# Three PSUM banks in turn for keys, values and expert products, and a new order for VectorE's side work

## What is computed

```
x = x + tanh(g_xattn[0]) * xattn0(ctx, layernorm(x), mask)      # 8 heads of 64
x = x + tanh(g_ffn[0])   * moe(layernorm(x))                    # 8 experts, 2 for each token
x = x + tanh(g_xattn[1]) * xattn1(ctx, layernorm(x), mask)      # 16 heads of 64
x = x + tanh(g_ffn[1])   * ffn1(layernorm(x))                   # 8-bit rows, ternary weights,
                                                                # depthwise convolution over 3 tokens, silu
```

## Time and profile before

| | |
|---|---|
| median of three runs | 1717.39 us |
| profiled execution: its own time | 1729.88 us |
| its span, first to last instruction | 1728.0 us |
| mean granted TensorE clock | 0.919 of full speed |
| TensorE busy | 1329.0 us, 77% |
| VectorE busy | 1171.2 us, 68% |
| ScalarE busy | 978.1 us, 57% |
| GpSimd busy | 867.0 us, 50% |

### The profile page before, as it was taken

One profiled execution on the slowest core, in us unless ns is written; L12 is line 12 of the kernel. 1 busy time (PEld: TensorE's weight loads), 2 busy tenths in 40 slices (PEclk: granted clock), 3 DMA queues, 4 the chain that ended last, 5 costly groups with the idle time before them and its releaser, 6 DMA issues.

```text
span 1728.0 us, 45307 instructions
## 1 busy us (share of the span) xinstructions
PE 1329.0 (77%) x16918; PEld 1016.7 (59%) x16918; DVE 1171.2 (68%) x3155; ACT 978.1 (57%) x2319; POOL 867.0 (50%) x1157
## 2 busy tenths in 40 slices
PE   2477777769888888788999888778777877877764
PEld 1355555547766766567877766555555655655553
DVE  4376768776655666656676667777777777767766
ACT  3466667446645666455545456556556655655651
POOL 4477667677755754555454443434333333433320
PEclk9798889889998999899999999999989999989985
DMA  4979978278999854479999963334234334423330
GB/s 130 255 187 187 222 166 201 64 194 202 242 203 234 198 82 91 108 188 210 236 235 241 227 150 64 72 80 85 61 76 88 67 69 80 80 66 72 72 61 9
DMA packets 443131, 239.97 MB, mean 139 GB/s; under 512 B 388784, under 2 KB 425760, under 8 KB 434336
## 3 DMA queue, kind: packets, MB, share of 16 engines
q1 hardware_dynamic: 407100, 172.49, 49.4%
q10 hardware_dynamic: 32740, 57.24, 11.0%
q0 software_dynamic: 3072, 7.34, 1.6%
HBM read 107.78 MB, written 35.50 MB: 83 GB/s over the span
## 4 chain that ended last, share of the span: by engine, by line
PE 28%; DVE 23%; ACT 14%; issue 10%; DMA 8%; POOL 8%; DVEq 5%; SPq 3%; ACTq 2%; another core or an unknown queue 0%; POOLq 0%
PE bank_keys L945 6%; PE bank_values L958 5%; ACT scores L740 4%; PE bank_hidden L995 4%; PE bank_x L1056 4%; POOL probs L580 3%; ACT probs L747 3%; DMA expert_up<-experts_up 3%; DMA probs_turned<-probs 3%; DVE scores L1205 3%; PE bank_out L977 2%; PE bank_scores L920 2%; DVE keys L1217 2%; ACT keys L760 2%; DVE values L1222 2%
## 5 line engine op out<-in xcount | busy, mean ns | idle before, releaser
L580 POOL TENSOR_TENSOR probs<-scores,probs 112x487 f16<-112x487 f32 x384 | 434.3, 1147 | 492.5 <-ACT probs L747 489.4
L740 ACT ACTIVATE scores<-scores,score_min 112x487 f32<-112x487 f32 x384 | 265.8, 694 | 182.1 <-DVE score_min L1205 181.0
L945 PE MATMUL bank_keys<-kv_B,weights 128*128 128x488 f16 x768 | 199.6, 401 | 102.6 <-DVE keys L1217 102.5
L1205 DVE CUSTOM_DVE_ANT_0 scores<-bank_scores,mask 112x487 f32<-112x487 f32 x384 | 238.7, 659 | 15.6 <-PE bank_scores L920 13.2
L958 PE MATMUL bank_values<-weights,kv_B 128*128 128x128 f16 x3072 | 199.2, 223 | 53.2 <-DVE values L1222 52.3
L747 ACT ACTIVATE probs<-scores 112x487 f16<-112x487 f32 x384 | 214.0, 605 | 24.1 <-DMA probs_turned<-probs 6.9
L958 PEld LDWEIGHTS bank_values<-weights,kv_B 128*128 128x128 f16 x3072 | 181.3, 100 | 73.5 <-DVE values L1222 72.9
L977 PE MATMUL bank_out<-values,probs_turned 128*128 128x64 f16 x4608 | 172.2, 195 | 8.7 <-DMA probs_turned<-probs 5.0
L1222 DVE SCALAR_TENSOR_TENSOR values<-bank_values,values 128x512 f16<-128x512 f32 x192 | 132.0, 687 | 62.7 <-ACT values L766 62.1
L945 PEld LDWEIGHTS bank_keys<-kv_B,weights 128*128 128x128 f16 x768 | 71.2, 103 | 174.7 <-DVE keys L1217 110.0
L977 PEld LDWEIGHTS bank_out<-values,probs_turned 128*128 128x128 f16 x4608 | 160.6, 100 | 10.6 <-issue 7.3
(11 more groups left out here) (225 smaller groups left out, 2382.8 us busy)
## 6 DMA issues: line engine op xcount, KB each, us to landing
expert_up<-experts_up SPq DMA_DIRECT2D x43, 1024.0 KB, 5.4
expert_down<-experts_down SPq DMA_DIRECT2D x43, 512.0 KB, 6.7
raw_weights<-in_weights ACTq DMA_DIRECT2D x8, 1536.0 KB, 10.6
experts_up<-expert_up ACTq DMA_DIRECT2D x8, 1024.0 KB, 5.5
raw_weights<-in_weights ACTq DMA_DIRECT2D x6, 1024.0 KB, 8.2
probs_turned<-probs SPq DMA_TRANSPOSE x384
context_turned_B<-kv_B ACTq DMA_DIRECT2D x16, 375.0 KB, 7.3
kv_B<-context_turned_B ACTq DMA_DIRECT2D x16, 375.0 KB, 3.8
```

The lines of the kernel that those rows point to most:

```text
L580: pool.tensor_tensor(PR[:, u % 4, 1, 0:KEYS], S[:, u % 4, 0:KEYS], PR[:, u % 4, 0, 0:KEYS], ALU.subtract).then_inc(probs_split, 1)
L740: act_e.activation(S[:, u % 4, 0:KEYS], S[:, u % 4, 0:KEYS], ACT.Exp, bias=rmin[:, u % 4:u % 4 + 1], scale=-1.0, accum_out=rsum[:, g % 2, ...
L945: last = pe.matmul(bK[:, 0:KW], w(wk + kb * step, a, 128 * (j % 4), 128), kv[layer][:, n % 2, kb, b, 0:KW], start=i == 0, stop=i == 5)
L1205: dve.tensor_tensor_reduce(out=S[:, u % 4, 0:KEYS], in0=bS[u % 2][0:TOK, 0:KEYS], in1=mask[:, m, 0:KEYS], scale=1.0, scalar=3.0e38, op0=AL ...
```

## The change

It has three parts.

1. **A ring of three banks.** Keys, values and the two expert halves take `bank_ring_0`, `_1`, `_2` in the order in which TensorE writes them (`ring_uses`). A use waits until the one three places before it has been read. Without experts this means that keys j+2 wait for the split of values j-2, and values j for the split of keys j+1. Three banks replace three, none is added.
2. **Evictions lag a place.** VectorE and ScalarE handle the `late` tasks of step j-1 in step j, not those of step j at its end. `split_k(j + 1)` comes right after the masks of step j, before it was `split_k(j + 2)` near the end of step j. `split_v(j - 1)` follows later; beside experts (`with_experts`) the values are split in their own step. VectorE does the `early` tasks behind its side work, ScalarE does them ahead of `round_probs`. The heads' and router's tasks come a step later where `slack` is 1 (all groups but two).
3. **The side work is dealt anew.** The tasks of the norms, the quantising and the convolution move to other steps, all still on VectorE. The eight taps of the convolution now stand in steps 18 and 19 of a sequence, before four in each of steps 16 to 19. The spill of a context to DRAM is issued a step later, the store of an expert tile a step earlier but behind the transposes.

```diff
+RING = 3
+def ring_uses():
+    uses = []
+    for j in range(FIRST_STEP, LAST_STEP + 1):
+        m = micro(j)
+        if is_pair(j + 2):
+            uses.append(("k", j + 2))
+        if m[0]:
+            uses.append(m[0])
+        if is_pair(j):
+            uses.append(("v", j))
+        if m[2]:
+            uses.append(m[2])
+    return uses
...
+            def ring_free(*use):
+                i = RING_AT[use] - RING
+                if i < 0:
+                    return
+                last = RING_USES[i]
+                if last[0] == "k":
+                    pe.wait_ge(k_split, last[1] + 1)
+                elif last[0] == "v":
+                    pe.wait_ge(v_split, last[1] + 1)
+                else:
+                    pe.wait_ge(gated, 2 * tile(last[1], last[2]) + last[3] + 1)
...
-                pe.wait_ge(k_split, j)
+                ring_free("k", j)
...
-                pe.wait_ge(v_split, j)
+                ring_free("v", j)
...
@@ early(j)
+    for n in range(NSEQ):
+        if j == start_b(n) + 26:
+            tasks.append(("f_down", n))
...
@@ late(j), where at = j - start_b(n)
-        if at == 14:
+        if at == 16:
             tasks.append(("f_turn", n))
-        if at == 15:
-            tasks.append(("f_up", n, 0))
-        if at == 24:
-            tasks.append(("f_max", n, 1))
-        if at == 27:
-            tasks.append(("f_down", n))
+        if at in (17, 18):
+            tasks.append(("f_up", n, at - 17))
+        if at in (20, 21):
+            tasks.append(("f_max", n, at - 20))
+        if at == 22:
+            tasks.append(("f_rate", n))
...
@@ ScalarE
-                if (j + 3) % 4 == 0 and 0 <= (j + 3) // 4 < NSEQ:
-                    spill_context((j + 3) // 4)
+                if (j + 2) % 4 == 0 and 0 <= (j + 2) // 4 < NSEQ:
+                    spill_context((j + 2) // 4)
...
+                for t in early(j):
+                    part(t)
                 if is_pair(j):
                     act_e.drain()
                     round_probs(2 * j)
                     round_probs(2 * j + 1)
                 load_weights(j)
-                for t in early(j):
+                for t in late(j - 1):
                     part(t)
...
@@ VectorE
-                    if at in (16, 17, 18, 19):
-                        f_conv(n, (at - 16) // 2, 1 + at % 2)
+                    if at in (18, 19):
+                        f_conv(n, at - 18, 1)
+                        f_conv(n, at - 18, 2)
```

More of the change, by code:

```diff
@@ L127, in early @@
         tasks.append(("wsum", 0))
-    for n in range(NSEQ):
-        at = j - start_b(n)
-        if at == 16:
-            tasks.append(("f_up", n, 1))
-        if at == 20:
-            tasks.append(("f_max", n, 0))
-        if at == 25:
-            tasks.append(("f_rate", n))
     return tasks
@@ L1519, in _ @@
                     mask_scores(2 * j + 1)
-                if is_pair(j - 1):
-                    split_v(j - 1)
+                if is_pair(j + 1) and not with_experts(j - 1):
+                    split_k(j + 1)
+                for t in late(j - 1):
+                    part(t)
+                for g in range(PAIRS // 4):
+                    if slack(g) and j == 4 * g + 6:
+                        norm_out(g)
                 if is_pair(j + 2):
                     split_q(j + 2)
-                for t in early(j):
-                    part(t)
-                if (j + 9) % 4 == 0 and 0 <= (j + 9) // 4 < NSEQ:
-                    p_norm((j + 9) // 4)
+                if is_pair(j - 1) and not with_experts(j - 1):
+                    split_v(j - 1)
+                for n in range(NSEQ):
+                    if j == p_step(n, -9, -12):
+                        p_norm_context(n)
+                    if j == p_step(n, -9, -11):
+                        p_norm_rest(n)
+                    if j == p_step(n, -8, -9):
+                        p_apply(n)
                 if -9 <= j < -7:
@@ L1560, in _ @@
                     split_l1_chunk(c)
+                if m[0]:
+                    gate_hidden(m[0][1], m[0][2], m[0][3])
+                for t in early(j):
+                    part(t)
+                for n in range(NSEQ):
+                    if j == 4 * n + 7 + slack(n):
+                        stats("M", n)
+                    if j == 4 * n + 8 + slack(n):
+                        m_apply(n)
                 for b in range(2):
@@ L1567, in _ @@
                         weigh_experts(b)
-                m = micro(j)
-                if m[0]:
-                    gate_hidden(m[0][1], m[0][2], m[0][3])
-                if is_pair(j + 2):
+                if with_experts(j) and is_pair(j + 2):
                     split_k(j + 2)
-                if is_pair(j - 2) and (j - 2) % 4 == 3:
-                    norm_out((j - 2) // 4)
-                for t in late(j):
-                    part(t)
+                for g in range(PAIRS // 4):
+                    if not slack(g) and j == 4 * g + 5:
+                        norm_out(g)
+                if with_experts(j):
+                    split_v(j)
                 if m[2]:
```

160 lines of the change are left out of this document (91 added, 69 removed).

## The result

The changed kernel takes 1769.37 us (median; 1755.71 to 1773.09) where the kernel before, on the same chip, takes 1721.2 (1716.7 to 1731.51): 1.026 times as long, 95% interval 1.018 to 1.033. I forecast 1681. The profiled execution has a span of 1768.4 us; before's was 1728.0.

The account below looks back on a forecast made before the run. Beside experts TensorE was taken as the bound; elsewhere, engines waiting for each other. Terms -7 - 24 - 5 - 7 + 3 + 4 = -36 us took the 1717.39 median to 1681, range 1645 to 1724.

Parts of the forecast that it names:

- start, to step 5's first mask: Kernel start: spill issued a step later no longer blocks ScalarE, values no longer wait for VectorE's split; -7 us.
- layer A, steps 5 to 30: Early layer A: per four steps, VectorE waits of 7.6 us go, TensorE waits of 3.0 come; -24 us.
- layer A beside experts: Layer A's expert steps: TensorE is the bound, 0.3 us saved a step; -5 us.
- gap: Steps 56 to 78, with few sides: a third of a microsecond saved from each; -7 us.
- layer B beside experts: TensorE-bound expert steps: steps 2 and 3 get the same wait, three periods, about 1.5 us each; +4 us.
- rest of layer B: Layer B outside experts: eight-step period goes from 60.25 to 60.5 us, times 10.75 periods; +3 us.
- end, after the last mask: Kernel end: a chain of single groups in the same order; 0 us.
- the clock: Layer B's period: two TensorE waits over 3 us bring slow stretches; +1.7 us a period.
- the walk: Layer B's eight steps, added up at full clock: 58.8 us, with step 2 at 10.1 and step 3 at 10.7.
- the prediction's own 2.4: Layer B's period in the kernel before: 2.4 us shorter if TensorE ran at 2.4 GHz all along.
- signs that I named: Right: layer A's 26 steps 195 to 205 us, layer B's period 59 to 62; wrong: period under 57 or over 63.
- slow rival: Layer B: both long TensorE waits bring full slow stretches, 63.5 us a period, +35, 1737 us in all; chance 0.18.

Follow-up runs that it names:

- filler: The changed kernel with 12 to 16 never-read TensorE products added in steps 2 and 3 of each layer B period outside the experts; 1753.57 us, ratio 1.022.
- taps_later: The changed kernel with the convolution's taps, and the FFN's work behind them up to `f_scale`, one step later; 1697.12 us, ratio 0.988.
- tail_prompt: The changed kernel with VectorE's early drains right behind `split_v` and `b_apply` ahead of the taps, in layer B's steps without experts; 1728.21 us, ratio 1.007.
- the ring alone: The kernel before, its order of work unchanged, with only the three banks used in turn; 1674.87 us, ratio 0.977.

## Why the prediction was wrong

The sum forecast -36 us; the two profiles differ by +40.4. Term by term, from the same two traces:

| term | forecast | measured |
|---|---|---|
| start, to step 5's first mask | -7 | +4.5 |
| layer A, steps 5 to 30 | -24 | -19.8 |
| steps 31 to 37 | not in the sum | -8.1 |
| layer A beside experts | -5 | +4.4 |
| gap | -7 | -1.3 |
| layer B beside experts | +4 | +20.7 |
| rest of layer B | +3 | +30.9 |
| end, after the last mask | 0 | +9.1 |

**The failed step is the period of layer B**, "two waits of TensorE over 3 us a period, as before has one of 5.4, so it gets slow stretches too: +1.7, 60.5". It is 64.16 in the period shown. Both long waits were found, with step 2 right to 0.35 us. Two terms of the sum were wrong: the clock, at 1.7 us, and contention for the moved side work, which I had put at nothing without a reason.

**The clock cost about 3.9 us.** In steps 2 to 4 the walk has 27.85 us, the filler 27.70 and the changed kernel 30.50: 2.8 us for the slow stretches behind the two waits. A third stretch stands behind a wait that I had not counted: in step 0 TensorE waits 2.89 us for `o_proj`'s drain. The filler adds no product there, and its rows show what follows at half clock:

```profile
1208.28 0.47 PE L1146 MATMUL bank_x<-identity_f,raw_weights 112*128 112x112 f32 x2 [2.89 <-DVE x L1537]
1208.78 1.25 PE L978 MATMUL bank_scores<-keys,queries 64*112 64x488 f16 x6
1210.50 2.37 PE L1004 MATMUL bank_ring<-kv_B,weights 128*128 128x488 f16 x6
```

Scores take 0.43 us more than at full clock, and the keys, 0.97 more, make the values of step 1 start 0.7 later: 1.1 us in all, which I read off these rows as an estimate. The rival in which both waits bring a full slow stretch has 4.7 us above the walk (1.7 and 3). It was nearer than my 1.7, and I gave it 0.18. Its 63.5 a period lies close to 64.16 partly by luck, since it has no contention in it.

**Contention cost about 1.5 us.** I had asked where the taps fall against GpSimd, and not where the other moved work falls. `f_round` moved from step 2 to step 0, where GpSimd splits the probabilities. The row of after, and its row of before:

```profile
L1487 DVE TENSOR_SCALAR context<-context 128x896 f16<-128x896 f32 x8 | 8.8, 1094 | 0.6
```
```profile
L1421 DVE TENSOR_SCALAR context<-context 128x896 f16<-128x896 f32 x8 | 5.0, 627 | 0.6
```

That is 0.47 us more on average and 0.75 in step 128 (1.38 us). In step 7 it is the normalisation of `f_apply` (L1332, before L1269) that now stands beside GpSimd, in each of the ten periods of the tail. The rows are duration minimum, median and maximum in ns, after and before:

```profile
L1332 DVE TENSOR_SCALAR raw_weights<-x,mean_var_F,rstd_F x10: 1048/1155/1160, 1072.2 to 1645.2; 112x256 f32<-112x256 f32 x10
```
```profile
L1269 DVE TENSOR_SCALAR raw_weights<-x,mean_var_F,rstd_F x12: 404/405/407, 1051.0 to 1694.8; 112x256 f32<-112x256 f32 x12
```

These 0.75 us are step 7's excess over the walk (7.27 for 6.5), as that step is VectorE's own work. So 2.2 more for the clock and 1.5 for contention make the 3.7 us between 60.5 and 64.16. Without its slow stretches the changed period would be about 60.3 us, and before's, by the prediction's own 2.4, about 57.9: the new order is longer there even at full clock. Both are estimates from the rows above.

**Layer B beside experts** is the same error in a stage that TensorE bounds. It isn't spread evenly: against before, steps 83, 91 and 99 (step 3 of a period) take 11.7 us more together, steps 80, 88 and 96 (step 0) 6.4, steps 84, 92 and 100 (step 4) 6.2, and steps 82, 90 and 98 (step 2) 0.6 less. Step 91 of the changed kernel:

```profile
874.01 2.22 DVE L1502 SCALAR_TENSOR_TENSOR context<-raw_weights,vectors,context 128x112 f32<-128x112 f32 x8 [4.15 <-ACT context L884]
...
877.30 0.62 DVE L1527 TENSOR_TENSOR heads_turned<-bank_x,heads_turned 128x448 f16<-128x448 f32 x1
...
877.97 0.63 PE L1103 MATMUL bank_x<-identity_f,x_normed 112*128 112x112 f32 x2 [3.90 <-DVE heads_turned L1527]
...
878.55 2.74 PE L1056 MATMUL bank_ring<-raw_weights,expert_up 128*128 128x128 f16 x24
...
881.22 1.47 PE L978 MATMUL bank_scores<-keys,queries 64*112 64x488 f16 x6
```

TensorE waits 3.90 us where I took 1.5, and then `up1` takes 2.74 where its fellow of the same step takes 1.50. That the place of the taps is the cause in step 3 of a period is shown by taps_later, which gives 17.5 us back in steps 83, 91 and 99. Another 14.5 of its 32.6 come from steps 82, 90 and 98, which were as long in the kernel before: that is a gain of its own. The 6 us of step 0 are not firm: the filler and tail_prompt, whose edits leave these steps alone, both have 4.3 less there.

**Layer A** was right in size (7.78 us a step; I said 7.6, and 195 to 205 us in all), and in what the change takes away: VectorE's waits for ScalarE's values and heads, 22.3 and 19.6 us in this stretch before, are down to 1.7 for the heads. What comes in their place was only partly what I had. TensorE waits 1.2 to 1.6 us before `p_turn` for `o_proj`'s drain in three sequences and 0.3 in a fourth, 4.5 us in all, where I had 1.9 in each, and before `p_lat` once, 2.7 us. A larger wait was not in the sum: the queries' products wait for GpSimd's work on the next sequence (L991, up to 3.9 us), 19.6 us in all against 6.9 before. My 3.0 us of added waits a sequence make 19.5 us in this stretch; of the kinds that I named 7.2 came. So about 12 us too much of one wait stand against 13 us of another that I didn't see, and that these sums nearly cancel is luck. **Beside experts** and **the gap** nothing came of the thirds of a microsecond; I had no row for them. The seven steps between the stretches, 31 to 37, gave 8.1 us that the sum left out.

**Start.** The spill's issue now blocks ScalarE for 3.46 us, not 9.76, and the values no longer wait: that step was right, though the reason that I gave, a queue that has emptied, is not shown. Step 1 is 10.9 us shorter for it, and steps 2 to 4 are 10.5 longer; in step 3 TensorE waits 4.55 us for the turned probabilities (the last line below), and what makes these late I didn't trace. The gain of step 1 is not larger for this reason: a drain of `p_turn`, ahead of the masks since late tasks are drained a step later, waits for GpSimd's half of the context, whose other half ScalarE makes behind the same long issue (the first line below); this link is read off the code. The other 4.3 us stand ahead of step 0: the first mask is that much later than before.

```profile
53.17 10.43 ACTq L738 DMA_DIRECT2D moe_rows<-moe_rows  x2
...
65.48 0.55 DVE L1518 COPY context_turned<-bank_x 128x375 f32<-128x375 f32 x1 [11.04 <-issue]
66.09 0.89 PE L1091 MATMUL bank_x<-identity_f,context 125*128 125x125 f32 x3 [10.07 <-DVE context_turned L1518]
...
73.69 3.46 ACTq L722 DMA_DIRECT2D context_turned_B<-kv_B  x1
...
89.25 0.82 PE L1037 MATMUL bank_out<-values,probs_turned 128*128 128x64 f16 x12 [4.55 <-DMA probs_turned<-probs]
```

**The end** isn't "the same order": with the last FFN's tasks one or two steps later than before, they stand in a chain with nothing beside them. From the last first mask to the end it is 68.0 us after, 58.9 before, 58.5 with the ring alone and 60.6 with taps_later.

Of the signs that I named, most came true: keys never wait, the heads' wait is gone, layer A in 195 to 205 us, steps 2 and 3 over 9.5 with TensorE waiting before `f_up` and `b_lat`. Two say wrong: values after the zeroing (a `p_turn` now waits in their place) and the period, over 63. Signs that hold don't make the time right where waits are priced too low and one is left out. The slow rival as a whole, 1737 us, was passed as well.

What stays open: how the 20.7 us beside the experts divide between idle and slow TensorE time, since the filler was not put there; what delays the first mask by 4.3 us and step 3 by its 4.55; and the layer A stage beside experts, which ran from 200 to 215 us among all these kernels with no clear tie to the edit.

## What to carry to other kernels

Price a long wait of TensorE as its length plus the groups behind it at half clock, once for each: here those of 2.9 to 4.5 us in the period had slow groups behind them, and the one of 0.8 us in step 2 had none. When side work is moved on an in-order engine, ask three things: does it wait for another engine in the same step, who waits for what is queued behind it, and beside whose memory traffic does it now fall? And split a large change before believing in it: here two pieces (three banks in turn, ScalarE's heads before its probabilities) gave 4.4%, and the new order around them gave it all back and 2.6% more.

## What the hardware showed that I had not expected

- Sixteen matmuls whose result nobody reads, put into each of two waits of TensorE, shortened a period from 64.16 to 61.40 us, and its granted clock rose from 0.89 to 0.97.
- Eight taps on VectorE take 2.25 us alone, and 3.81 to 3.92 beside GpSimd's split of the probabilities (2.2): starting them 1.2 us earlier made them end later.
- VectorE's `tensor_scalar` of 112x256 f32 takes 0.41 us on VectorE alone and 1.16 us beside the same split, though the prediction had priced this only for the taps.
- An early `combine` waited 3.14 us for gathers that one longer step had hidden before: cover that is counted in steps shrinks when a step gets short.
